# Thirteen small loads of the set-up moved to ScalarE's DMA queue, and a final copy in rows of 16 KB

## The reference

```
x = x + tanh(g_xattn[0]) * attention(layernorm(x), ctx, Wq, Wkv, null_kv, Wout, ln_scale, ln_bias)   # 16 heads of 64
x = x + tanh(g_ffn[0])   * ffn(layernorm(x), w1, b1, w2, b2)      # relu, values quantized to 8 bits
x = x + tanh(g_xattn[1]) * depool(rmsnorm(layernorm(x)) @ W_in.T + b_in, rmsnorm(ctx), patch lengths)
x = x + tanh(g_ffn[1])   * experts(layernorm(x), router, gating_w, linear_w, per_expert_scale)     # top 2 of 8
```

## Time and profile before

| what | value |
|---|---|
| median of 3 runs | 1680.04 us (1680.03 to 1680.61) |
| the profiled execution's own time | 1678.45 us |
| its span, first to last instruction | 1676.7 us |
| busy share TensorE, VectorE, ScalarE, GpSimd | 89%, 71%, 55%, 35% |
| mean granted TensorE clock | 0.964 of full |
| DMA moved | 98.12 MB in 77836 packets |

### The profile page before, as it was taken

The page is one execution under the profiler, slowest core; times in us unless marked ns, Lnnn a source line. Parts: engine busy times, 40 slices in busy tenths (PEclk is TensorE's granted clock), DMA queues, the critical chain, the costliest instruction groups (busy, mean ns, idle before and its releaser), DMA issues.

```text
span 1676.7 us, 35791 instructions
## 1 busy us (share of the span) xinstructions
PE 1493.0 (89%) x12510; PEld 1085.1 (65%) x12510; DVE 1195.3 (71%) x3240; ACT 922.1 (55%) x2526; POOL 589.2 (35%) x775
## 2 busy tenths in 40 slices
PE   3799999999999999999999999999765499999994
PEld 2567676767767676767767676776553266666662
DVE  5478788888878888887978888887763344445442
ACT  4276666767666676767666676766641133333331
POOL 3011333242323333232333324232333356555552
PEclk9899999999999999999999999999877699999997
DMA  7201021020202012020201102010400363333334
GB/s 249 70 1 64 14 64 58 20 77 2 77 8 71 26 52 71 7 76 1 77 14 64 65 14 77 2 58 8 164 32 0 105 173 61 60 59 58 58 61 123
DMA packets 77836, 98.12 MB, mean 59 GB/s; under 512 B 20400, under 2 KB 61376, under 8 KB 77600
## 3 DMA queue, kind: packets, MB, share of 16 engines
q1 hardware_dynamic: 51152, 77.01, 14.1%
q0 software_dynamic: 15680, 18.69, 6.8%
q10 hardware_dynamic: 10832, 0.13, 0.3%
HBM read 64.89 MB, written 35.10 MB: 60 GB/s over the span
## 4 chain that ended last, share of the span: by engine, by line
PE 62%; DVE 18%; ACT 7%; POOL 5%; issue 3%; SPq 2%; DMA 2%; ACTq 0%; POOLq 0%; DVEq 0%
PE S L1282 11%; PE W L949 9%; PE W L951 9%; PE W L950 9%; PE T L954 7%; PE O L1302 6%; PE O L1053 4%; POOL routing_table L693 4%; PE S L1027 3%; DVE mx L1462 3%; ACT prob L785 2%; DVE pTl L1474 2%; PE W L954 2%; PE W L1158 2%; PE W L1138 2%
## 5 line engine op out<-in xcount | busy, mean ns | idle before, releaser
L785 ACT ACTIVATE prob<-S,nm 128x256 f32<-128x256 f32 x512 | 235.5, 474 | 80.8 <-DVE nm L1465 54.1
L778 ACT ACTIVATE pTh<-T 128x512 f16<-128x512 f32 x256 | 139.3, 597 | 137.1 <-PE T L954 136.9
L634 POOL TENSOR_SCALAR ve_ln<-mv_ln 128x2 f32<-128x2 f32 x64 | 14.6, 229 | 472.8 <-DVE mv_ln L1436 471.9
L1462 DVE TENSOR_REDUCE mx<-S 128x2 f32<-128x512 f32 x256 | 163.3, 679 | 21.2 <-PE S L1027 20.7
L1282 PE MATMUL S<-GL,xgh 128*128 x568 | 169.8, 381 | 2.7 <-DVE xgl L1756 2.7
L1474 DVE SCALAR_TENSOR_TENSOR pTl<-T,pTh 128x512 f16<-128x512 f32 x256 | 164.1, 682 | 6.4 <-ACT pTh L778 6.4
L716 POOL DMA_INDIRECT acc_rows<-ysb,tab x71 | 112.3, 1582 | 134.2 <-DMA acc_rows<-ysb,tab 90.3
L794 ACT ACTIVATE prob<-prob,rden 128x256 f32<-128x256 f32 x256 | 116.5, 504 | 56.4 <-DVE p0n L1483 55.7
L954 PE MATMUL T<-ident,prob 128*128 128x128 f32 x1024 | 141.5, 282 | 1.8 <-DVE prob L1487 1.7
L949 PE MATMUL W<-cTh,Wkh 128*128 128x256 f16 x512 | 140.6, 275 | 0.0
L950 PE MATMUL W<-cTl,Wkh 128*128 128x256 f16 x512 | 140.5, 274 | 0.0
(11 more groups left out here) (293 smaller groups left out, 4325.1 us busy)
## 6 DMA issues: line engine op xcount, KB each, us to landing
cx<-in_ctx_dram SPq DMA_DIRECT2D x16, 512.0 KB
gst<-in_L_ffn_gating_w_dram SPq DMA_DIRECT2D x16, 512.0 KB
gating_split<-gsp SPq DMA_DIRECT2D x16, 512.0 KB
GL<-gating_split SPq DMA_DIRECT2D x8, 1024.0 KB
stg<-in_L_xattn_Wkv_dram SPq DMA_DIRECT2D x8, 512.0 KB, 13.5
xl<-in_x_dram SPq DMA_DIRECT2D x16, 256.0 KB
lst<-in_L_ffn_linear_w_dram SPq DMA_DIRECT2D x16, 256.0 KB
xres<-in_x_dram SPq DMA_DIRECT2D x16, 256.0 KB
```

The source lines that it names most:

```text
L778: A(flat(pTh[:, h, :, :]), T[h][:, :], ACT.Copy).then_inc(s_pTh[h], 1)
L785: ins = A(prob[:, h, t, :], S[h][:, t * NTOK:(t + 1) * NTOK], ACT.Exp, bias=nm[:, h, t:t + 1], scale=SM, accum_out=rs[:, h, t:t + 1])
L1462: ins = V.tensor_reduce(mx[:, h, :], S[h][:, :].rearrange("p (t k) -> p t k", t=TT), AX.X, ALU.max)
```

## The change

1. The thirteen loads of `later` are issued by ScalarE on its queue, right behind the five of `small` and ahead of its first chunk. SP no longer issues them.
2. SP loads the first batch's `xl` behind `wis`, ahead of chunks 6 to 11, not behind `cx`.
3. ScalarE's wait for `s_later` and the tanh stand behind `high(3)`, not behind `high(9)`.
4. VectorE's wait for the tanh and its ten small operations stand behind `low(5)`, not behind `low(9)`.
5. Each half of the final copy is described as 128 rows of 16 KB, not as 2048 rows of 1 KB.

```diff
@@ SP
                 if n == 5:
                     sp.dma_start(wis[:, :, :], wi_v).then_inc(s_nat[2], 16)
-            for dst, src in later:
-                sp.dma_start(dst, src, allow_slow_non_contiguous=True).then_inc(s_later, 16)
+                    sp.dma_start(xl[0][:, :, :], x_v[0]).then_inc(s_x[0], 16)
             sp.dma_start(cx[0][:, :, :], ctx_v[0]).then_inc(s_c[0], 16)
-            sp.dma_start(xl[0][:, :, :], x_v[0]).then_inc(s_x[0], 16)
             sp.wait_ge(s_const, 1)
...
                 rows = slice(h * NTOKENS // 2, (h + 1) * NTOKENS // 2)
-                sp.dma_start(out.rearrange("b n d -> (b n) d")[rows, :], acc_d[rows, :]).then_inc(s_out[h], 16)
+                sp.dma_start(out.rearrange("b n d -> (b n) d")[rows, :].rearrange("(p r) d -> p (r d)", p=P),
+                             acc_d[rows, :].rearrange("(p r) d -> p (r d)", p=P)).then_inc(s_out[h], 16)
@@ ScalarE
                 act.dma_start(dst, src, allow_slow_non_contiguous=True).then_inc(s_small, 16)
+            for dst, src in later:
+                act.dma_start(dst, src, allow_slow_non_contiguous=True).then_inc(s_later, 16)
...
                 high(n)
-                if n == len(chunks) - 3:
+                if n == 3:
                     act.wait_ge(s_later, 16 * len(later))
                     A(tg[:, :], graw[:, :], ACT.Tanh).then_inc(s_tanh, 1)
@@ VectorE
             for n in range(3, len(chunks) - 2):
                 if n not in POOL_CHUNKS:
                     low(n)
-            dve.wait_ge(s_tanh, 1)
-            link(V.tensor_scalar(tgs[:, :], tg[:, :], 1 / WS, None, ALU.mult))
...
-            link(V.tensor_copy(bq_b[:, :], o16[:, 0, :]))
+                if n == 5:
+                    dve.wait_ge(s_tanh, 1)
+                    link(V.tensor_scalar(tgs[:, :], tg[:, :], 1 / WS, None, ALU.mult))
...
+                    link(V.tensor_copy(bq_b[:, :], o16[:, 0, :]))
```

More of the change, by code:

```diff
@@ L1387, in _ @@
                     low(n)
-            dve.wait_ge(s_tanh, 1)
-            link(V.tensor_scalar(tgs[:, :], tg[:, :], 1 / WS, None, ALU.mult))
[L1390 to L1397, removed]
-            link(V.tensor_copy(bq_b[:, :], o16[:, 0, :]))
+                if n == 5:
+                    dve.wait_ge(s_tanh, 1)
+                    link(V.tensor_scalar(tgs[:, :], tg[:, :], 1 / WS, None, ALU.mult))
+                    V.tensor_scalar(sc_b[:, :], sc_b[:, :], tg[:, 0:1], None, ALU.mult)
+                    V.tensor_scalar(bi_b[:, :], bi_b[:, :], tg[:, 0:1], None, ALU.mult)
+                    V.tensor_scalar(bin_b[:, :], bin_b[:, :], tg[:, 2:3], None, ALU.mult)
+                    V.tensor_scalar(gi_b[:, :], gi_b[:, :], BCOEF * WS, None, ALU.mult)
+                    V.tensor_scalar(pes[:, :], pes[:, :], tgs[:, 3:4], None, ALU.mult)
+                    for k in range(KD):
+                        V.tensor_scalar(rw[:, k, :], rw[:, k, :], rsc[:, k:k + 1], D ** -0.5, ALU.mult, ALU.mult)
+                    link(V.tensor_copy(o16[:, 0, :], bq_b[:, :]))
+                    link(V.tensor_copy(bq_b[:, :], o16[:, 0, :]))
             for n in (len(chunks) - 2, len(chunks) - 1):
```

## The result

The changed kernel takes **1691.45 us** (median of 6 runs, 1688.19 to 1692.31) where the kernel before, on the same chip, takes 1680.9 (6 runs): ratio 1.006, 95% interval 1.0047 to 1.0073. It is slower by about 10 us. The forecast was 1685.4. The direction and the wait for the small loads were forecast, the length of the work behind that wait was not. The median lies 0.95 us beyond the upper end of the range, 1690.5. The profiled execution took 1691.97 us, span 1690.2.

What follows compares the result with a forecast made beforehand. The prediction took the set-up as bound by late small loads, and batch loop and expert tiles by TensorE. It added +5.4 (set-up) and 0 (final copy) to 1680.04, giving 1685.4 us; range 1674.0 to 1690.5, the forecast's own 1681.6 to 1690.5.

Steps and rivals of the forecast that it cites:

- Part 1: Set-up, thirteen small loads on ScalarE's queue: advancing at the pace of SP's packets, the last is in at 36.8 us.
- The turns: Set-up DMA: two queues with work alternate packet for packet, whatever the packet size, so both show equal packet counts.
- Part 2: Set-up, tanh after the fourth chunk: remaining chunk work waits for the loads; batch work at 50.7 us against 45.34, +5.4.
- T: Set-up: the time when the last of the thirteen small loads is in, forecast at 36.8 us; break-even at 31.4.
- the small operations 2.25: VectorE's small operations after the tanh in the set-up, counted at 2.25 us in all.
- T+14.8: VectorE's set-up work ends 14.8 us after the small loads are in, counting slower chunks beside GpSimd; T+13 without slowing.
- Part 3: Thirteen more issues ahead of ScalarE's first chunk: it starts at 13.1 us, price zero; if held up, up to +10.5.
- Part 4: SP's queue in the set-up: cx, the table's fill and the later Wout product stay covered and cost nothing.
- Part 5: Final copy at the program's end, in 16 KB packets: between -1.4 and +1.1 us, taken as 0.
- 1 (the loads slip through): Set-up rival, chance 0.25: small loads are in by 26 us or less, -6 us, 1674.0 us.
- 2: Set-up rival, chance 0.15: loads in between 29 and 33 us, or ScalarE starting at 18 to 22; no change, 1680 us.
- 3: Final copy rival, chance 0.05: 16 KB packets cost more each, 4.8 us more while the set-up stays even, 1684.8 us.

Runs made afterwards that it cites:

- tanh_only: The kernel before with only the tanh moved behind ScalarE's fourth chunk and VectorE's small operations behind chunk 5; loads stay on SP's queue. Ratio 1.0071.
- vector_late: The changed kernel with VectorE's ten small operations back in their old place behind all Wkv chunks. Ratio 1.0049 against the kernel before.
- split: The kernel before with only the five repeated rows and pes on ScalarE's queue; the seven tiny loads stay on SP's. Ratio 1.001.
- loads_only: The kernel before with only the thirteen loads moved to ScalarE's queue; tanh, small operations and xl in their old places. Ratio 1.0034.
- pieces16k: The kernel before with the final copy viewed so that neighbouring rows can't be joined, giving 256 packets of 16 KB. Ratio 1.0005.

## Why the prediction was wrong, step by step

- **Part 1 held.** The loads were to be in at 36.8 us, the tanh ran at 37.97. The turns showed in both stretches above (76 and 77, 111 and 110 packets). That the sum came so near is in part luck: the tiny packets were through at about 24 us, not 25.4, and the last six loads took some 14 us, not 11.4.
- **Part 2 failed in its tail.** The prediction put T+13.9 for the way from the tanh to the batch work. It measured 17.56 here and in tanh_only. The mis-sized term is "the small operations 2.25": 8.1 us, +5.85, since this time they stand beside GpSimd's chunk work. (They are ten; the prediction counts nine, with the right time for all.) The three chunks behind them took 3.5 instead of 5.7, -2.2, as GpSimd was done by then, and chunk 5 took 1.25 instead of 1.9. From the longer of the two counts, T+14.8, that leads to T+17.8. Taking 13.9, between the two, missed 0.9 more. I had taken the price of the small operations from a row in which GpSimd was idle and had counted its slowing for the chunks alone. The rows here say that such an operation can last until GpSimd's TENSOR_TENSOR ends: sc_b 2.30 us in the changed kernel, 2.29 in tanh_only, vector_late and split, 0.35 wherever GpSimd was done. The Trainium skill has a rule for this (page "SBUF — State Buffer", section "Who interferes with whom"): VectorE shares one pair of ports with GpSimd, copy, cast and tensor_scalar can take it, and whoever holds it keeps it for the whole instruction, while an operation with at most one SBUF input outside the two-port modes does not contend. Beside a TENSOR_TENSOR the trace agrees: 2.30 us with an SBUF input, 0.48 with a bank's. Beside GpSimd's TENSOR_SCALAR it agrees only in part: bin_b ran there at its ordinary 0.34 us, bi_b took 1.12. The runs don't show in which mode an operation ran, so that the ports are the reason is argued; that GpSimd's work beside it is the cause is shown.
- **Sum of the set-up.** T came 1.2 us later than forecast and the tail was 3.7 longer: 55.5 us for 50.7, +10.2 instead of +5.4. This is the miss. The range was left for a smaller reason: its upper end, +10.5, would have held the set-up's +10.2, but it was counted from 1680.04, and with three more runs the kernel before has a median of 1680.9, to which the measured time is +10.55.
- **Part 3, price zero, was right for this kernel and wrong as a reading of the queue.** One issue was held up for 8.53 us and the first chunk came at 21.67, not at 13.1; the prediction had this case, a first chunk at 20 to 30 us, as its high end, and a first chunk after 20 us as a sign of being wrong. That sign came true and was not what set the time: by the prediction's count a start at 21.67 gives 21.67 + 25.9 = 47.6 us, less than the 55.5 that T led to. Alone the hold-up is worth 5.9 us: loads_only starts at 23.45, which by the same count gives 49.4, and 51.20 was measured; its six chunks beside GpSimd took 2.1 us longer than before. That the later of the two counts decides is shown by the parts, which don't add up.
- **Part 4 held.** cx and the fill cost nothing; TensorE did the product with Wout from 38.59 in 6.53 us at a granted clock of 1.00 (4.93 us before, at 1.00 too), and the batch work again began at half: 0.50 from 53 to 62 us.
- **Part 5 had the right number from a wrong premise.** It assumed that the pieces exist. They don't, and when they do (pieces16k) the last landing is about 1 us later, which the whole time doesn't show (1.0005).
- **Rivals.** 1 (the loads slip through) was refuted by the equal counts. 2 had two conditions, and one came true, ScalarE at 18 to 22 us (21.67); no change did not follow, since the other wait was later. 3 fell with the copy. The rival that was missing is that the tail behind T is longer than its rows say.

## What to carry to other kernels

Before a wait is moved ahead of work that its delay used to cover, count that work by what will run beside it in the new place: the durations in the old rows belong to the old neighbours. A load that reads one row for every partition was slow here on either queue, and on the second queue it slowed the first; loading the row once and spreading it by a product with ones was faster. Where two waits run side by side, taking away the earlier one gains nothing, so find out first which of them ends last.

## What the runs showed of the hardware that I had not expected

- Loads that read one 1 KB row of DRAM for 128 partitions moved 62 GB/s, 59 packets of 1 KB and more a microsecond; 128 different rows of the same size moved 220 GB/s, 212 a microsecond.
- Two queues with work took turns, packet for packet (76 and 77, 111 and 110, 204 and 205), and this works against the faster one: the weights fell from 0.40 to 0.15 MB/us beside repeated rows.
- ScalarE's queue held its issuer up when much was outstanding: 8.53 us in one issue in the changed kernel, 8.64 in loads_only, 9.32 in vector_late, the thirteenth of each; the twelve ahead took 0.4 to 0.9. In split, with eleven issues in all, there was no such stop.
- VectorE's plain operations on SBUF (tensor_scalar, cast) could last until a TENSOR_TENSOR of GpSimd ended (0.35 us became up to 2.30), its scalar_tensor_tensor chunks only slowed down (1.2 to 2.1), and reads from a PSUM bank were not touched (0.48 and 0.48). Beside a TENSOR_SCALAR of GpSimd one operation took 1.12 us and the next its ordinary 0.34; why is open.
- Rows of 16 KB that follow one another in a DRAM to DRAM copy went as 64 KB packets in either description.
